# Two experts start on images 0 to 3 while the tokens of images 4 to 7 are still being chosen

## The reference

```python
affinity = jax.nn.softmax(logits, axis=-1).transpose(0, 2, 1)
gating, index = jax.lax.top_k(affinity, k)              # k = 1024 // 16 * 2 = 128
x_in = jnp.take_along_axis(x[:, None, :, :], index[..., None], axis=2)
h = jax.nn.gelu(jnp.einsum('bekd,edh->bekh', x_in, w1) + b1[None, :, None, :])
x_e = jnp.einsum('bekh,ehd->bekd', h, w2) + b2[None, :, None, :]
weighted = gating[..., None] * x_e
out = out.at[jnp.arange(Bx)[:, None], idx_flat].add(vals_flat)
```

## Time and profile before

| what | us |
|---|---|
| median of three runs | 3197.95 |
| the profiled execution | 3197.93 |
| its span in the trace | 3196.1 |
| PE busy | 3062.6 (96%) |
| DVE busy | 2291.5 (72%) |
| ACT busy | 1850.8 (58%) |
| POOL busy | 1093.3 (34%) |
| attention ends, `experts` begins at about | 2356.8 |
| first expert product of PE begins at | 2413.26 |

### The profile page before, as it was taken

The page is one execution under the profiler, slowest core; times in us unless marked ns, Lnnn a source line. Parts: engine busy times, 40 slices in busy tenths (PEclk is TensorE's granted clock), DMA queues, the critical chain, the costliest instruction groups (busy, mean ns, idle before and its releaser), DMA issues. The chain is left out here.

```text
span 3196.1 us, 49855 instructions
## 1 busy us (share of the span) xinstructions
PE 3062.6 (96%) x18116; PEld 2629.6 (82%) x18116; DVE 2291.5 (72%) x3580; ACT 1850.8 (58%) x3353; POOL 1093.3 (34%) x1113
## 2 busy tenths in 40 slices
PE   6999999999999999999999999999938999999998
PEld 5988889888878888888888888889826888888886
DVE  5878688678768876886888788678764655655653
ACT  3876678477747756783876578478712333333332
POOL 1225123412513251342225123412513444444443
PEclk9999999999999999999999999999978999999999
DMA  7122221321231232113213221311134566566564
GB/s 237 37 60 106 65 60 51 116 68 37 71 122 37 64 116 64 54 57 106 68 43 107 84 60 44 113 51 37 41 116 109 123 147 142 121 145 143 122 145 59
DMA packets 121614, 283.60 MB, mean 89 GB/s; under 512 B 22464, under 2 KB 30656, under 8 KB 110656
## 3 DMA queue, kind: packets, MB, share of 16 engines
q1 hardware_dynamic: 92736, 213.72, 20.2%
q0 software_dynamic: 28672, 67.13, 11.9%
HBM read 173.08 MB, written 74.15 MB: 77 GB/s over the span
## 5 line engine op out<-in xcount | busy, mean ns | idle before, releaser
L802 DVE TENSOR_TENSOR PT<-ring,PT 128x512 fp32r<-128x512 f32 x1024 | 676.5, 686 | 161.0 <-ACT PT L535 142.6
L535 ACT ACTIVATE PT<-ring 128x512 fp32r<-128x512 f32 x1024 | 582.9, 598 | 170.7 <-PE ring L929 87.5
L961 PE MATMUL O<-PT,V 128*128 128x256 f32 x4096 | 673.3, 289 | 0.0
L734 DVE TENSOR_REDUCE nmax<-S 128x1 f32<-128x1024 f32 x512 | 619.7, 1211 | 54.2 <-PE S L918 54.1
L929 PE MATMUL ring<-ident,prob 128*128 128x128 f32 x4096 | 614.1, 273 | 16.3 <-DVE PT L802 12.9
L961 PEld LDWEIGHTS O<-PT,V 128*128 128x128 f32 x4096 | 575.5, 189 | 40.3
L918 PE MATMUL S<-kd,qs 128*128 128x512 f32 x2048 | 599.1, 414 | 2.1 <-ACT prob L526 1.7
L526 ACT ACTIVATE prob<-S,nmax 128x1024 f32<-128x1024 f32 x512 | 571.1, 1115 | 36.0 <-DVE nmax L734 36.0
L464 POOL COPY oS<-oHL 64x256 f32<-64x256 f32 x256 | 100.8, 394 | 1283.6 <-ACT oHL L584 1278.1
L929 PEld LDWEIGHTS ring<-ident,prob 128*128 128x128 f32 x4096 | 464.3, 139 | 55.7 <-issue 48.9
L918 PEld LDWEIGHTS S<-kd,qs 128*128 128x128 f32 x2048 | 347.1, 189 | 50.4 <-issue 5.3
(11 more groups left out here) (132 smaller groups left out, 3461.5 us busy)
## 6 DMA issues: line engine op xcount, KB each, us to landing
kd<-kd SPq DMA_DIRECT2D x128, 256.0 KB, 3.7
wraw<-w_dram SPq DMA_DIRECT2D x32, 1024.0 KB, 7.0
wqk<-wqk_split SPq DMA_DIRECT2D x24, 1024.0 KB, 4.8
xt<-x_dram SPq DMA_DIRECT2D x16, 1024.0 KB, 7.8
Rs<-rinv_rows SPq DMA_DIRECT2D x56, 256.0 KB, 3.4
PT<-wv_split SPq DMA_DIRECT2D x7, 2048.0 KB, 8.8
oT<-x_dram SPq DMA_DIRECT2D x24, 512.0 KB, 3.3
out_dram<-oT SPq DMA_DIRECT2D x48, 256.0 KB, 8.2
```

Of the source, the lines that this page charges most:

```text
L535: nc.scalar.activation(PT[:, 0, u // 2 % 2, 4 * c:4 * c + 4, u % 2 * P:u % 2 * P + P], ring[:, k % 2, :].rearrange("p (m q) -> p m q", m=4 ...
L734: nc.vector.tensor_reduce(nmax[:, s:s + 1], S[:, s % 2, :], AX.X, ALU.max, negate=True).then_inc(max_done, 1)
L802: nc.vector.tensor_tensor(PT[:, 1, here[0], here[1], here[2]], ring[:, k % 2, :].rearrange("p (m q) -> p m q", m=4), PT[:, 0, here[0], her ...
L961: last_mm = nc.tensor.matmul(O[:, m % 2, 0:QC], V[:, t, head // 2, 2 * (head % 2):2 * (head % 2) + 2, :].rearrange("p h d -> p (h d)"), PT ...
```

## The change

Experts 0 and 1 both visit images 0 to 3 first and then both visit images 4 to 7: v = 0 is expert 0 on images 0 to 3, v = 1 expert 1 on images 0 to 3, v = 2 and v = 3 the same experts on images 4 to 7. From expert 2 on the order is as before. These four visits are written out; v = 0 and v = 1 have a program of their own, in which ACT makes the high parts of h and of the weights and POOL the low parts (DVE makes the low part of expert 0's w1 only), and the 48 picking instructions of the second set stand between DVE's other work. All eight chunks of expert 2's weights are split by DVE in v = 3. Loads of w1 and w2 are counted apart (`w1_in`, `w2_in`); in the loop they wait for the split chunks alone, and only the biases wait for `y0_done`. The choice's transposes go to `xr` and no longer to `p2`.

```diff
         @block.sync
+            load_w1(0)
             for h in range(2):
                 sp.dma_start(work[HROWS * h:HROWS * h + HROWS, :], half_rows(aff_dram, HB, h)).then_inc(aff_in, 16)
-            load(0, 0)
-            sp.wait_ge(ws_lo, WCH)
-            load(1, 1)
+            load_w2(0)
+            load_biases(0, 0)
+            sp.wait_ge(first_w1_lo, KC)
+            load_w1(1)
+            sp.wait_ge(ws_lo, split_chunks(0))
+            load_w2(1)
...
+            with sp.Fori(1, E // 2 - 1) as twos:
                 for k in range(2):
                     e = 2 * twos
-                    sp.wait_ge(ws_lo, (e + k) * WCH + 2 * WCH)
+                    sp.wait_ge(ws_lo, (e + k) * WCH + 2 * WCH - KC)
                     sp.sem_inc(sp_passed2, 1)
+                    load_w1(e + k + 2)
+                    load_w2(e + k + 2)
                     sp.wait_ge(y0_done, (e + k) * (2 * G) + 2 * G)
-                    load(e + k + 2, k)
+                    load_biases(e + k + 2, k)
...
         @block.gpsimd
+            def low_of_h(v):
+                for m in range(KC):
+                    pool.wait_ge(h_hi, v * KC + m + 1)
+                    nc.gpsimd.tensor_tensor(hT[:, 1, m, :], hf[:, m % 2, :], hT[:, 0, m, :].bitcast(F32),
+                                            ALU.subtract).then_inc(h_lo, 1)
+            pool.wait_ge(chosen, 2)
+            early_gather(0)
+            low_of_weights(0, KC)
+            early_gather(1)
+            low_of_h(0)
+            low_of_weights(1, 0)
+            early_scatter(0)
+            low_of_h(1)
             pool.wait_ge(chosen, 4)
-            columns(0, 0)
-            pool.wait_ge(cols_made, 1)
-            gather(0, 0)
-            gather(0, 1)
-            every_expert(pool, expert)
+            early_gather(2)
+            early_scatter(1)
+            early_gather(3)
...
         @block.scalar
+            for c in range(KC):
+                high_of_weights(0, c)
             for j in range(G):
                 turn(0, 0, j)
+                high_of_weights(0, KC + j)
+            act.wait_ge(b12_in[0], 32)
+            for m in range(KC):
+                gelu(0, 0, m)
+                high_of_h(0, m)
+            high_of_weights(1, 0)
+            high_of_weights(1, 1)
+            for j in range(2):
+                turn(1, 1, j)
+                high_of_weights(1, 2 + j)
+            act.wait_ge(chosen, 2)
+            for j in range(G):
+                if j < 2:
+                    turn(1, 1, 2 + j)
+                early_weigh(0, j)
+                high_of_weights(1, KC + j)
...
         @block.vector
             join_halves(0)
-            dve.wait_ge(aff_in, 32)
-            for n in range(PICKS):
-                pick_step(nc, dve, n, work[:, :], best_b, pos_b, picked_b)
+            for c in range(KC):
+                dve.wait_ge(ws_hi, c + 1)
+                nc.vector.tensor_tensor(ws[:, 0, 1, c, :], wraw[:, c, :], ws[:, 0, 0, c, :].bitcast(F32),
+                                        ALU.subtract).then_inc(first_w1_lo, 1)
+            for j in range(G):
+                turn(0, 0, j)
+                pick(j, j + 1)
+            pick(G, 18)
+            turn(1, 1, 0)
+            turn(1, 1, 1)
+            pick(18, 21)
+            for j in range(G):
+                if j in (1, 2):
+                    turn(1, 1, 1 + j)
+                add_b2(0, 0, j)
+                pick(21 + j, 22 + j)
+            pick(25, PICKS)
             dve.wait_ge(picked_b, PICKS * 2 // 3)
             reverse_second_half(1, best_b, pos_b)
+            add_b2(1, 1, 0)
             join_halves(1)
+            for j in range(1, G):
+                add_b2(1, 1, j)
...
+            for v in (2, 3):
+                for m in range(KC):
+                    split_h(v, m)
+                    if v == 3:
+                        split_chunk(2, 0, m)
...
+                    add_b2(v, v % 2, j)
+                    if v == 3:
+                        split_chunk(2, 0, KC + j)
...
         @block.tensor
+            turn_choice(0)
+            pe.wait_ge(rows_made, 1)
             for j in range(G):
                 turn(0, 0, 0, j)
+            pe.wait_ge(first_w1_lo, KC)
+            project_1(0, 0, 0)
...
+            pe.wait_ge(ws_lo, split_chunks(0) + KC)
+            project_1(1, 1, 1)
+            pe.wait_ge(ws_lo, split_chunks(1))
+            for j in range(G):
+                if j == 2:
+                    turn_choice(1)
+                project_2(1, 1, j)
+            pe.wait_ge(rows_made, 2)
+            for j in range(G):
+                turn(1, 2, 0, j)
```

More of the change, by code:

```diff
@@ new lines, in low_of_h, with low_of_weights @@
+            def low_of_h(v):
[3 more added lines that the diff above has]
+                                            ALU.subtract).then_inc(h_lo, 1)
+            def low_of_weights(e, c0):
+                for c in range(c0, WCH):
+                    pool.wait_ge(ws_hi, e * WCH + c + 1)
+                    nc.gpsimd.tensor_tensor(ws[:, e, 1, c, :], wraw[:, c, :], ws[:, e, 0, c, :].bitcast(F32),
+                                            ALU.subtract).then_inc(ws_lo, 1)
@@ L1307, in expert @@
                     for m in range(KC):
[L1308 to L1312, removed]
+                        gelu(v, k, m)
                     more = not (last and g == 1)
@@ L1319, in expert @@
                             turn(v + 1, 1 - g, 2 + j)
[L1320 to L1321 removed]
+                        if type(e) is int and e == 2 and g == 0:
+                            act.wait_ge(added[G + j], 16)
+                        else:
                             act.wait_ge(added[G * g + j], e * 16)
[L1323 to L1328, removed]
+                        weigh(v, g, j, gatec[:, k, G * g + j:G * g + j + 1])
+            for c in range(KC):
+                high_of_weights(0, c)
             for j in range(G):
                 turn(0, 0, j)
[L1331 removed]
+                high_of_weights(0, KC + j)
[14 more added lines that the diff above has]
+                high_of_weights(1, KC + j)
+            act.wait_ge(b12_in[1], 32)
+            for m in range(KC):
+                gelu(1, 1, m)
+                high_of_h(1, m)
+            for j in range(G):
+                early_weigh(1, j)
+            for j in range(G):
+                turn(2, 0, j)
+            act.wait_ge(chosen, 4)
+            for v in (2, 3):
+                for m in range(KC):
+                    gelu(v, v % 2, m)
+                for j in range(2):
+                    turn(v + 1, 1 - v % 2, j)
+                for j in range(G):
+                    if j < 2:
+                        turn(v + 1, 1 - v % 2, 2 + j)
+                    early_weigh(v, j)
+            later_experts(act, expert)
         @block.vector
@@ L1417, in join_halves, with pick @@
                                         ).then_inc(chosen, 1)
+            def pick(n0, n1):
+                if n0 == 0:
+                    dve.wait_ge(aff_in, 32)
+                for n in range(n0, n1):
+                    pick_step(nc, dve, n, work[:, :], best_b, pos_b, picked_b)
             reverse_second_half(0, best_a, pos_a)
@@ L1486, in _ @@
+            turn_choice(0)
+            pe.wait_ge(rows_made, 1)
             for j in range(G):
                 turn(0, 0, 0, j)
-            every_expert(pe, expert)
+            pe.wait_ge(first_w1_lo, KC)
+            project_1(0, 0, 0)
+            turn(0, 1, 1, 0)
+            turn(0, 1, 1, 1)
+            pe.wait_ge(ws_lo, split_chunks(0))
+            for j in range(G):
+                if j in (1, 2):
+                    turn(0, 1, 1, 1 + j)
+                project_2(0, 0, j)
+            pe.wait_ge(ws_lo, split_chunks(0) + KC)
@@ L1491 @@
+            later_experts(pe, expert)
 _OUT = "out_dram"
```

242 lines of the change are left out of this document (165 added, 77 removed).

## The result

The changed kernel takes 3168.2 us (median of 4 runs, 3166.47 to 3169.52) against 3197.11 us for the kernel before on the same chip (4 runs): a ratio of 0.9908, 95% interval 0.9896 to 0.992 (not quite the quotient of these two medians, 0.991). The forecast was 3169 us. The profiled execution took 3169.52 us, with a span of 3167.7.

What follows compares the result with a forecast made beforehand. TensorE was taken as idle before the first expert product while DVE makes 48 picks, then as the bound itself. 20.6 us up to expert 2 plus 8.5 later, 29.1 off 3197.93, gives 3168.8, forecast 3169; range 3159 to 3180 (8 in 10).

Steps and rivals of the forecast that it cites:

- first product starts: First visit: gathers land by 2368.5, turning four blocks takes 6.9 us, so the first expert product starts at 2375.4.
- length of that product: First visit's first product: 13.99 us, as before, since PE is as cold, with clock 0.50 before it.
- transposes of the choice: Second visit: PE reaches them at 2422.4, held by POOL's low parts of h, 0.8 after DVE's reversed halves at 2421.6.
- expert 2: Start of expert 2, after four early visits: at 2491.2 instead of 2511.82, 20.6 us won.
- a stall of 1.84 us: End of the fourth visit: PE waits 1.95 us for DVE's eighth weight chunk, behind the fourth addition of b2.
- the first gather: First visit's gathers: fourth issued 4.0 us after the first, landing 3.71 later, 4.7 at longest; taken as landed by 2368.5.
- my estimate from it, 1.2 us: First visit's last gathered block, at half rate beside the loads: 1.2 us more, the sum then 3170.0 instead of 3168.8.
- the third visit's restart: Third visit: PE nearly idle for 11 us before it, so a cold start is charged: 26.7 us, not 24.47.
- POOL's four low parts: Second visit: low parts of h start after the scatters end at 2413.5; the fourth is done at 2419.0.
- DVE's idle stretch ahead of the second visit's first block: DVE waits from 2386.1 to 2392.6 for the block ACT delivers behind the last gelu: 6.5 us idle.
- The later experts' 8.5 us: Later experts: 11.2 us of waits shrink to 2.7 through loads 1.5 us earlier and DVE awaiting w1 alone; 8.5 won.
- the first rival: Later experts win nothing, as earlier loads collide with the visit's end scatters and land as late: 3177.3 us, chance 0.13.

Runs made afterwards that it cites:

- e5: Changed kernel with the 48 picks back in one row on DVE right behind the first choice; 3196.3 us, ratio 1.0.
- e3: Changed kernel with the first visit's four scatters moved on POOL behind the low parts of the second visit's h; 3169.96 us, one run.
- e4: Changed kernel with the load of expert 1's w1 held until the first four gathers have landed; 3166.43 us, one run.
- e8: Changed kernel with expert 1's w1 held, picks in DVE's idle time, second choice's transposes inside second visit's first product, expert 2's chunks split over two visits; 3153.82 us, ratio 0.9865.
- e1: Changed kernel with loop loads of w1 and w2 again behind the last addition of b2, still counted apart; 3170.08 us, ratio 0.9917.
- e7: Changed kernel with picks filling DVE's two idle stretches, and POOL's low parts of h and third visit's gathers ahead of the first visit's scatters; 3168.52 us, one run.
- e6: Kernel before, with only w1 and w2 counted on two semaphores, loads issued where they were; 3187.9 us, ratio 0.9973.
- e2: Changed kernel with early loads, but DVE waits for both w1 and w2 before the first chunk; 3174.31 us, ratio 0.9925.

## Why the prediction was right

Times from the shared event, predicted (its own clock less 2357.91) and measured:

| step | predicted | measured |
|---|---|---|
| first product starts | 17.5 | 20.36 |
| length of that product | 13.99 | 12.60 |
| POOL's last low part of h | 61.1 | 62.13 |
| transposes of the choice | 64.5 | 65.71 |
| third visit | 80.8 | 81.49 |
| third visit's length | 26.7 | 25.38 |
| fourth visit's length | 25.8 | 25.87 |
| expert 2 | 133.3 | 132.74 |
| won behind it | 8.5 | 8.29 |

- The mechanism of the start held in each step: the picks hide beside the first two visits (e5: 26.4 us), POOL comes last at the transposes of the choice and the picks are done 0.72 us before it (0.8 predicted; e3 shows the order), the pipeline of the second visit sets the third, and a stall of 1.84 us (1.95 predicted) stands ahead of expert 2.
- The term that was mis-sized is the first gather: I took 3.7 to 4.7 and it took 7.04. I read the earlier trace rows as gathers beside loads and scatters, and for the loads that was wrong: no gather there goes out less than 11.8 us behind a load of w1, and the earlier trace rows has both loads landed within 10.3 of their issue. The excess is 3.3 us, of which e4 takes 2.0 away by moving one load. The rule of the Trainium skill (DMA: Bandwidth & Descriptors, Queues, rings and completion order) that the engines alternate between queues by packet points the same way; my estimate from it, 1.2 us, which I left out of the sum, was too small for it.
- Three terms erred the other way and covered it. The first product was 1.4 us shorter than before's; the second visit was 0.9 shorter (35.65 against 36.5), more than half of it between the transposes and the third visit (15.78 against 16.3); and the third visit's restart cost 1.7 us (25.38 against 23.68 in e8) instead of 3.1. That they cancel to 0.6 us at expert 2 is luck: with the same code the first product took 13.88 us in e1, and the third visit 23.79.
- Two details of the working: the 0.69 put down to rows 5 stands in the earlier trace rows, and the steps named for POOL's four low parts (1.28, twice 1.31, 1.28) add up to 5.2 us, not to the 5.5 used; measured were 5.4. DVE's idle stretch ahead of the second visit's first block was 4.85 us (6.5 predicted); a longer one, 8.85 us ahead of its first turn while the gathers land, the prediction doesn't name, and e7 and e8 put picks into it.
- The later experts' 8.5 us were right in size, but the working credited two causes together, earlier issue and separate counting. The second is enough for all of it (e1, e6). The earlier issue adds nothing to it: most of the 1.5 us is lost in longer landings, as the first rival had it, though not shown to be for the rival's reason, the scatters. Alone, with one wait for both loads, it keeps 3.15 of the 8.3 us (e2; 4.7 if expert 2's slow first product is left out).

## What to carry to other kernels

Where an engine's serial work stands ahead of the bound engine, spread it in pieces over that engine's idle time; then look for who ends last next, since here POOL, the picks and PE's own order stood within 2 us of each other, and only moving all of them at once gained much (about 10 of e8's 14 us lie between the first product and the third visit). Give each load that is used at its own time its own count before issuing it earlier: the count was worth 8.5 us alone, the issue nothing beside it. And price a gather from rows that have the same loads beside it.

## What the runs showed of the hardware

- A gather of 128 rows lands in 3.5 to 3.8 us in the kernel before at its first choice, and in 5.5 to 7.0 in after, beside 1 MB loads; with one of them held back (e4) 5.0 to 6.6. In e1, e2 and e3, with after's code up to there, the range is 5.4 to 7.6.
- The granted clock in front of the third visit differs between executions of nearly the same work. The last 5.87 us before the visit, and its first 4.60, in after:

```profile
2434.64:2440.51 5.87, 3.90 (x16) 2.96 (x16) 2.77 (x4) 2.39 (x4) 4.96 (x4) 0.50 0.98 125
2440.51:2445.11 4.60, 4.60 (x13) 3.71 (x14) 0.00 (x0) 0.00 (x0) 3.42 (x7) 0.63 0.95 231
```

and in e4, where PE had stood idle for about as long ahead of the first turn (3.92 us, against 4.04 in after):

```profile
2433.23:2439.10 5.87, 3.47 (x17) 2.73 (x17) 2.70 (x4) 2.39 (x4) 4.96 (x4) 0.71 1.01 124
2439.10:2443.70 4.60, 4.60 (x20) 3.83 (x21) 0.75 (x2) 0.69 (x1) 3.69 (x5) 1.00 0.94 207
```

At 0.50, the lower level of 1.2 GHz, the visit takes 25.38 us; where the clock had risen before it, 23.75 (e4) and 23.79 (e1). What decides it is open: these kernels differ there in little but time, the idle stretch was 4.14 us in e1 (where the clock rose) and 3.88 in e2 (where it did not), and no run was made for it. The same holds for the stall of 1.84 us ahead of expert 2: in e2 the clock in the 4.60 us behind it was 0.63, in after, e1, e3, e4, e5 and e7 it was 1.00.
